# Code-book layer: for half of the sub-spaces the gates go through DRAM and come back with each row on 32 partitions

## The reference, cut to what matters

```python
B, T, D = (2, 512, 192)            # here the layer gets 16 tiles of 128 tokens, 2048 tokens in all
S, R, M, K = (8, 16, 64, 4)        # 8 sub-spaces of 16 features, 64 codes each, the best 4 are kept
H, G = (32, 64)                    # 32 hidden features per code
z = jnp.einsum('nd,sdr->nsr', xf, P)
scores = jnp.einsum('nsr,smr->nsm', z, C)
topv, topi = jax.lax.top_k(scores, K)
w = jax.nn.softmax(topv, axis=-1)
...
h = jax.nn.gelu(jnp.einsum('nsr,nskrh->nskh', z, W1g) + b1g)
yl = jnp.einsum('nskh,nskhr->nskr', h, W2g) + b2g
comb = jnp.einsum('nskr,nsk->nsr', yl, w)
out = jax.nn.gelu(comb @ G1 + g1b) @ G2 + g2b
```

## Time and profile before

| | before |
|---|---|
| median of 3 runs (lowest, highest) | 3582.79 us (3580.55, 3584.8) |
| profiled execution: own time | 3578.07 us |
| its span, first to last instruction | 3576.3 us |
| mean granted TensorE clock, share of full speed | 0.83 |
| PE, DVE, ACT busy over the span | 71%, 68%, 45% |
| loop over the 128 steps, about | 2291 to 2813 us |

### The profile page before, as it was taken

One profiled execution on the slowest core, in us unless ns is written; L12 is line 12 of the kernel. 1 busy time (PEld: TensorE's weight loads), 2 busy tenths in 40 slices (PEclk: granted clock), 3 DMA queues, 4 the chain that ended last, 5 costly groups with the idle time before them and its releaser, 6 DMA issues. The chain is left out here.

```text
span 3576.3 us, 39626 instructions
## 1 busy us (share of the span) xinstructions
PE 2556.9 (71%) x13085; PEld 1566.8 (44%) x13132; DVE 2419.3 (68%) x5733; ACT 1604.6 (45%) x2888; POOL 831.2 (23%) x438
## 2 busy tenths in 40 slices
PE   3968995788888876699831113788989777785466
PEld 3955663333434333499621111322222366664345
DVE  4454336399999997211378996687787699998621
ACT  1111112566666652111217772677777545554211
POOL 1000000467676762367200001000000011111021
PEclk9768997899999997799955555899999888887678
DMA  1121001202020200511100001000000100000221
GB/s 37 19 80 45 1 1 31 91 4 95 0 95 0 95 0 1 165 40 40 46 10 0 1 1 44 13 1 1 1 1 1 30 1 1 1 1 1 67 110 50
DMA packets 59444, 109.35 MB, mean 31 GB/s; under 512 B 32045, under 2 KB 47755, under 8 KB 53995
## 3 DMA queue, kind: packets, MB, share of 16 engines
q1 hardware_dynamic: 53484, 95.04, 8.2%
q0 software_dynamic: 5760, 11.82, 1.1%
HBM read 92.76 MB, written 18.03 MB: 31 GB/s over the span
## 5 line engine op out<-in xcount | busy, mean ns | idle before, releaser
L1938 POOL TENSOR_TENSOR mam_st<-mam_du,mam_b_rows 128x1536 f32<-128x1536 f32 x128 | 439.5, 3441 | 172.7 <-PE mam_ysum L2007 172.2
L2168 DVE TENSOR_TENSOR_SCAN mam_st<-mam_da,mam_st 128x512 f32<-128x512 f32 x384 | 441.0, 1204 | 35.9 <-ACT mam_da L2108 18.2
L1716 DVE TENSOR_TENSOR cod_hp<-cod_hp,cod_gate 128x512 f32<-128x512 f32 x512 | 324.2, 682 | 123.0 <-ACT cod_hp L1583 121.0
L2007 PE MATMUL mam_ysum<-mam_st,held_ident 128*128 128x512 f32 x768 | 391.5, 650 | 2.2 <-DVE mam_st L2174 2.2
L1583 ACT ACTIVATE cod_hp<-cod_up,cod_b 128x512 f32<-128x512 f32 x512 | 319.2, 693 | 130.7 <-PE cod_up L1454 130.1
L2108 ACT ACTIVATE mam_da<-mam_delta,mamw_decay 128x508 f32<-128x508 f32 x384 | 254.1, 683 | 184.2 <-DVE mam_st L2168 149.5
L2282 POOL TENSOR_TENSOR att_probs<-att_se,att_neg 128x1536 f32<-128x1536 f32 x16 | 55.0, 3440 | 999.7 <-DVE att_neg L2487 999.7
L2174 DVE TENSOR_TENSOR mam_st<-mam_st,mam_c_ps 128x1536 f32<-128x1536 f32 x128 | 224.4, 1753 | 16.9 <-PE mam_c_ps L2002 13.4
L2007 PEld LDWEIGHTS mam_ysum<-mam_st,held_ident 128*128 128x128 f32 x768 | 159.9, 208 | 168.6 <-issue 161.5
L489 DVE SCALAR_TENSOR_TENSOR held_h<-x_dn,held_gate,held_h 128x192 f32<-128x192 f32 x256 | 89.1, 410 | 183.8 <-PE x_dn L456 182.1
L1459 PE MATMUL cod_gate<-cod_wt,cod_sel_g 128*128 128x512 bf16 x465 | 181.6, 391 | 39.4 <-DVE cod_hp L1716 38.8
(11 more groups left out here) (523 smaller groups left out, 5484.2 us busy)
## 6 DMA issues: line engine op xcount, KB each, us to landing
mam_b_rows<-b_scratch SPq DMA_DIRECT2D x32, 1024.0 KB, 6.8
sw_w<-in_L_w SPq DMA_DIRECT2D x2, 4608.0 KB, 33.2
gr_w<-in_L_w SPq DMA_DIRECT2D x1, 5376.0 KB, 43.3
gr_w<-in_L_w SPq DMA_DIRECT2D x1, 4608.0 KB
slot_scratch<-in_slot_fresh SPq DMA_DIRECT2D x1, 3860.0 KB
gr_rows<-slot_scratch SPq DMA_DIRECT2D x40, 96.5 KB, 1.9
x1w_w<-in_L_w SPq DMA_DIRECT2D x1, 3072.0 KB
gr_w<-home_scratch SPq DMA_DIRECT2D x16, 192.0 KB, 4.4
```

The lines of the kernel that those rows point to most:

```text
L1716: nc.vector.tensor_tensor(at, at, gate[u % BANKS][:], ALU.mult).then_inc(gated, 1)
L1938: nc.gpsimd.tensor_tensor(st[it % N_ST][:], du[r % 2][:], along(b_rows[:, p % RING, n % PIECE, :], 1, [P, MC, MT]), ALU.mult)\
L2007: last = nc.tensor.matmul(ysum[:, c, :], m.ident[:], st[it % N_ST][:, c, :], start=False, stop=(it % DS == DS - 1))
L2168: nc.vector.tensor_tensor_scan(fs, fa, fs, 0.0, ALU.mult, ALU.add).then_inc(scanned, 1)
```

## The change

The sub-spaces of a step fall in two halves. For j = 0 and 1 (QP = 2) gates are made as before. For j = 2 and 3 (QD = 2) there is no gate matmul. Instead, once for each group:

- PE transposes the fp32 gates `ex` of these sub-spaces (`turn_gates`, eight 128 x 128 transposes, at k = 23 and 24), and ACT copies them to `turned_gates`, 128 x 2 x 512 fp32.
- SP stores them to DRAM, `gate_scratch[g % 2]`, by four DMAs of 64 rows x 2,048 bytes (`send_gates`, behind the bring of k = 28).
- SP brings, for each step, a buffer of `wide_gates`, 128 partitions x 4,096 bytes (512 KB), out of a ring of GRING = 5 (`bring_gates`). The source is listed as 4 codes x 32 repeats (stride 0) x 4,096 bytes, and the destination as 128 partitions x 4,096 bytes. A bring waits until the step five earlier is gated.
- DVE multiplies `hp` with `wide_gates` for j = 2 and 3, and waits for the bring's semaphore `gates_in`.

There are now 4 `up` banks and 2 `gate` banks. The splitting in bf16 parts runs over half as many columns, `turn_w` is done four times per group in place of eight (k = 25 to 28), and the second bias is added through `turned_gates` for the one half (`b2d`, two fp32 matmuls) and as before for the other. Group 0's gates are transposed and sent ahead of the loop. The raw first-layer weights are loaded into `wide_gates` in place of `wt[1]`.

```diff
-BANKS = 3
+BANKS = 4
+GBANKS = 2
 HOLD = 3
+QP = 2
+QD = QS - QP
+NSP = 2 * QP
+GRING = 5
+SEND_AT = 28
...
 def code_of(k, j):
-    return (k % HT + 2 * j) % HT
+    return (k % HT + 2 * j) % HT if j < QP else k % HT
...
+            def send_gates(g):
+                if g == 0:
+                    sp.wait_ge(first_kept, FIRST_GF + 2)
+                else:
+                    sp.wait_ge(misc_kept, prep_turn(g) + GF_AT + 2)
+                for half in range(2):
+                    for j in range(QD):
+                        sp.dma_start(m.gate_scratch[g % 2, half].rearrange("c e j t -> (c e) j t")[:, j],
+                                     turned_gates[j * SM:(j + 1) * SM, half, :]).then_inc(gates_out, 16)
+
+            def bring_gates(g, k):
+                step = g * STEPS + k
+                if step >= GRING:
+                    sp.wait_ge(gated, QS * (step - GRING + 1))
+                sp.dma_start(wide_gates[:, step % GRING].rearrange("p j t -> p (j t)"),
+                             along(m.gate_scratch[g % 2, k // HT, k % HT].rearrange("e j t -> e (j t)"), 1,
+                                   [ET, SH, QD * GT])).then_inc(gates_in[step % GRING], 16)
+
+            sp.wait_ge(w1_split, 1)
+            send_gates(0)
+            for g in range(NG):
+                sp.wait_ge(gates_out, 16 * 2 * QD * (g + 1))
+                for k in range(STEPS):
+                    bring_gates(g, k)
+                    if k == SEND_AT and g + 1 < NG:
+                        send_gates(g + 1)
...
+            def turn_gates(g, half, bank, ready):
+                pe.wait_ge(weighted, GS * (g + 1))
+                for t in range(GS):
+                    at = t * SS + half * QS + QP
+                    last = nc.tensor.transpose(bank[:, t * P:(t + 1) * P],
+                                               ex[:, at:at + QD, :].rearrange("p n e -> p (n e)"), m.ident[:])
+                last.then_inc(ready, 1)
...
-                if u >= BANKS:
-                    pe.wait_ge(gated, u - BANKS + 1)
+                if j >= QP:
+                    return
+                if u >= QS:
+                    pe.wait_ge(gated, u - QS + 1)
...
-                        if 24 <= k:
-                            keep(turn + WT_AT + k - 24, turned_to(g + 1, k - 24), turned_from(misc))
+                        if 23 <= k < 25:
+                            keep(turn + GF_AT + k - 23, turned_gates[:, k - 23, :], misc[:])
+                        if 25 <= k < 29:
+                            keep(turn + WT_AT + k - 25, turned_to(g + 1, k - 25), turned_from(misc))
...
                 v.wait_ge(h_ready, u + 1)
-                v.wait_ge(gate_ready, u + 1)
                 at = hp[step % HOLD][:, j, :]
-                nc.vector.tensor_tensor(at, at, gate[u % BANKS][:], ALU.mult).then_inc(gated, 1)
+                if j < QP:
+                    v.wait_ge(gate_ready, QP * step + j + 1)
+                    by = gate[j][:]
+                else:
+                    v.wait_ge(gates_in[step % GRING], 16 * (step // GRING + 1))
+                    by = wide_gates[:, step % GRING, j - QP, :]
+                nc.vector.tensor_tensor(at, at, by, ALU.mult).then_inc(gated, 1)
...
+        m.gate_scratch = nc.dram_tensor("gate_scratch", [2, 2, HT, ET, QD, GT], F32).ap()
```

More of the change, by code:

```diff
@@ L1322, in codes_stage @@
         w2 = s.sb("w2", [P, SS * HT, SR])
-        b2_part = [s.sb(f"b2_part{i}", [P, 2 * SS, 32], BF16) for i in range(NPART)]
+        b2_part = [s.sb(f"b2_part{i}", [P, 2 * NSP, 32], BF16) for i in range(NPART)]
+        b2d = s.sb("b2d", [P, 2, 32])
         g1 = s.sb("g1", [P, 2, SG])
@@ L1346, in codes_stage @@
         up = [s.psum(f"up{i}", [P, 512]) for i in range(BANKS)]
-        gate = [s.psum(f"gate{i}", [P, 512]) for i in range(BANKS)]
+        gate = [s.psum(f"gate{i}", [P, 512]) for i in range(GBANKS)]
         comb = s.psum("comb", [P, 512])
@@ L1356, in codes_stage @@
          comb_kept, b2_ready, dve, act_own) = (s.sem(n) for n in names)
-        N_IN = 9
+        gates_out = s.sem("gates_out")
+        gates_in = [s.sem(f"gates_in{i}") for i in range(GRING)]
+        N_IN = 10
         block = s.block()
@@ L1420, in turn_w @@
                 turned = bank[:].bitcast(BF16)
-                for n in range(SS):
-                    last = nc.tensor.transpose(turned[:, n * P:(n + 1) * P], cols[:, t * 2 * SS + h * SS + n, :],
+                for n in range(2 * NSP):
+                    last = nc.tensor.transpose(turned[:, n * P:(n + 1) * P], cols[:, t * 2 * NSP + n, :],
                                                m.bf_ident[:])
@@ L1455, in unit @@
                                  start=True, stop=True).then_inc(up_ready, 1)
[L1456 to L1457 removed]
+                if j >= QP:
+                    return
+                if u >= QS:
+                    pe.wait_ge(gated, u - QS + 1)
                 half, code = f // NBLK, f % NBLK
[L1459 removed]
+                nc.tensor.matmul(gate[j][:], sel_g[:, code, :], wt[g % 2][:, 2 * (QP * (k // HT) + j) + half, :],
                                  start=True, stop=True).then_inc(gate_ready, 1)
@@ L1467, in down @@
                     for q in range(2 * NPART):
[L1468 to L1471, removed]
+                        for j in range(QP):
+                            n = 2 * (QP * half + j) + q % 2
+                            nc.tensor.matmul(comb[32 * j:32 * j + 32, :], b2_part[q // 2][:, n, :],
+                                             wt[g % 2][:, n, :], start=(q == 0), stop=False)
+                    for j in range(QD):
+                        rows, at = slice(j * SM, (j + 1) * SM), 32 * (QP + j)
+                        nc.tensor.matmul(comb[at:at + 32, :], b2d[rows, half, :], turned_gates[rows, half, :],
+                                         start=True, stop=False)
                 pe.wait_ge(gated, QS * (step + 1))
@@ L1492, in _ @@
                 spread_w1(i, first_turn(first_w(i)))
-            for i in range(2 * GS):
-                turn_w(0, i, first_turn(FIRST_WT + i), first_ready)
+            for half in range(2):
+                turn_gates(0, half, first_turn(FIRST_GF + half), first_ready)
+            for t in range(GS):
+                turn_w(0, t, first_turn(FIRST_WT + t), first_ready)
             pe.wait_ge(first_kept, N_FIRST)
@@ L1607, in _ @@
                         high_w(0, t)
+            for half in range(2):
+                keep_first(FIRST_GF + half, turned_gates[:, half, :], lambda bank: bank[:])
             for t in range(GS):
                 mid_w(0, t)
-            for i in range(2 * GS):
-                keep_first(FIRST_WT + i, turned_to(0, i), turned_from)
+            for t in range(GS):
+                keep_first(FIRST_WT + t, turned_to(0, t), turned_from)
             act.wait_ge(w_in, 16 * N_IN)
```

49 lines of the change are left out of this document (29 added, 20 removed).

## The result

The changed kernel takes 3727.1 us (median of 4 runs, 3721.8 to 3732.1), the kernel before 3581.7 us in the same series (4 runs, 3579.5 to 3584.8). The ratio is 1.0405, with a 95% interval of 1.0389 to 1.0421. The forecast was 3712 us, range 3672 to 3810, with 0.84 on slower. The profiled run of the changed kernel is 3723.8 us long, with a span of 3721.9 us. The stage, from its first DMA issue to the next stage's first reduction, grew from 598.6 us (2222.91 to 2821.55) to 747.2 us (2219.08 to 2966.29), by 148.6 us; all other stages together are 3.0 us shorter.

What follows compares the result with a forecast made beforehand. Brings on 4 of 16 DMA engines were to bound the loop: start 2286 + 655.4 brings + 4.1 sends + 1.2 gating + 8.6 tail = 2955.3, +133.8 us on 3578.07, giving 3712 us, range 3672 to 3810.

Steps and rivals of the forecast that it cites:

- The mechanism: Brings: equal parts must cut source's 4 and destination's 128 at their outermost counts, so 4 of 16 DMA engines serve them.
- rival 1: Brings: cut by the destination's 128 over 16 engines, 1.2 us each; DVE bounds; 3491 us, -87 us; chance 0.15.
- The price of a bring: Each step's transfer: 32 rows on each of four engines, 160 ns per 4,096-byte row, 5.12 us.
- rival 2: Brings: 4 engines at the 108-row loads' 19.9 GB/s, 6.59 us each, 3900 us; chance 0.04 together with anything beyond 3810.
- first issue of the stage to the first step's gates: Stage's prologue: group 0's gates copied by 2281.4, stored, bring data flowing from 2286, then the first bring; 68.2 us.
- 127 steps at the regular pace: Loop: the brings' queue never empties, so every step takes a bring's 5.12 us; 650.2 us.
- stores and irregular steps: Loop at a group's change: three later sends cost only their bytes, 3 x 524,288 at 388 GB/s, 4.1 us.
- last gating to the next stage's first reduction: Stage's tail behind the loop: 8.6 us, as in the trace before the change.
- rival 3: PE's clock in the loop: hidden unless below 0.62; mean 0.6 adds 20 us, 3732 us; no chance of its own.
- SP's issues: SP issuing DMAs in the loop: some 0.5 us each, hidden.
- Five buffers, four brings always queued: Bring queue in the loop: five buffers keep four brings queued, so it never empties and the loop runs at its pace.
- 405 us of work, perhaps 30 of stalls: DVE over the loop if 16 engines serve the brings: 435 us in place of 522, -87 us.

Runs made afterwards that it cites:

- e1: Changed kernel with each bring cut into four DMAs of one code each (source 1 x 32 repeats), same bytes and rows: 3523.0 us, ratio 0.984 to the kernel before.
- e2: Changed kernel with each bring cut into two DMAs of two codes each, so each source list has an outermost count of 2: 4377.2 us (one run).
- e3: Changed kernel with the bring's source listed as 32 repeats x 4 codes, still one DMA, constants permuted alike: 3520.8 us, ratio 0.983 to the kernel before.
- e6: Changed kernel with brings of half the bytes: as many descriptors on 4 engines, each 2,048 bytes: 3523.1 us, ratio 0.984 to the kernel before.
- e5: Changed kernel with gates stored to DRAM for the first group alone, the later stores and SP's waits for them left out: 3730.5 us.
- e4: Changed kernel with one bring per group, 124 of 128 transfers left out, every step of the group using that buffer: 3523.3 us (one run).

## Why the prediction was right

**The mechanism** was right: the count of engines was read from the packets of DMAs with equal lists and carried to a pair of unequal ones, 4 and 128, by the argument that equal parts must cut both. e1, e2 and e3 show it for 1 x 32, 2 and 32. The trace of before could not exclude rival 1, since all its lists were cut alike; e3, which differs from the changed kernel in nothing else of the transfer than the order of the source's list, does. What isn't shown is the rule in full. In these pairs the source has the smaller or an equal count and every destination's count is a multiple of 16, so "the largest common divisor up to 16" and "the source's count, up to 16" give the same for them; the 13 and 12 of the earlier trace rows speak for divisors, and a destination with the smaller count was not tried.

**The price of a bring** was put at 5.12 us and measures 5.08: 131,072 bytes per engine in 5.08 us are 25.8 GB/s, between the 24.3 and 26.6 GB/s of the earlier trace rows. It rested on the right neighbours, and the straight line through them held (e6). The bound of 6.59 us from the 108-row loads was far off, as was judged, and rival 2 with it.

**The sum** was 133.8 us for the stage, against 148.6 measured. It fell short by 14.8 us, in four terms (the two units behind the last step's gates, 1.2 us put and 1.3 measured, are not listed):

| term | predicted | measured | difference |
|---|---|---|---|
| first issue of the stage to the first step's gates | 68.2 | 73.8 | +5.6 |
| 127 steps at the regular pace | 650.2 | 645.2 | -5.0 |
| stores and irregular steps | 4.1 | 14.2 | +10.1 |
| last gating to the next stage's first reduction | 8.6 | 12.7 | +4.1 |

The first row is a sum of small things: the gates are copied 0.8 us later than put, the stores land later by about 1.6 us, and the first bring, issued at 2283.49, is gated at 2292.91, 9.4 us later, where 0.9 + 5.1 us were put. Of the 9.4, 1.4 us pass before its first packet and 7.3 until its last mark. The -5.0 of the second row takes back a quarter of what the others add. The third row is the term that was mis-sized. It held the stores alone, which was right for them (3 to 4 us by e5), and took every other step as regular. Of the 14.2 us, 3.9 are the steps 28, 60 and 92, the stores; 7.8 are eight single steps, told of in the last section; the remaining 2.4 are the net of steps at long preparation and the shorter ones behind them. The last row is rival 3's clock at a place where I hadn't looked for it. The down matmuls behind the last gating, eight of them, took 1.05 us in the earlier trace rows; here:

```profile
2953.69 1.91 PE L1528 MATMUL cod_comb<-cod_hp,cod_w 128*16 128x512 f32 x8 [3.16 <-DVE cod_hp L1782]
```

The granted clock of this stretch is 0.50, 1.2 GHz in place of 2.4, and it stays there to the stage's end, where the kernel before has 1.00:

```profile
2955.70:2966.30 10.60, 6.94 (x12) 3.03 (x12) 1.11 (x3) 1.24 (x2) 0.00 (x0) 0.50 0.00 0
```

PE had been idle for 3.16 us ahead of these matmuls. The matmuls of the tail take 1.91, 3.65, 1.65 and 1.65 us, and took 1.05, 1.90, 0.92 and 0.92: together 4.1 us more, the whole of the row. Inside the loop the slower clock is hidden, as argued: the mean granted clock is 0.85, PE is busy 477 of 668 us. But behind the loop nothing hides it, and the tail is paid at the low clock.

**SP's issues** were put at 0.5 us each and hidden. They are hidden, but they aren't 0.5 us long (last section). "Five buffers, four brings always queued" was not quite so; about three and a half were, which was enough.

**Rival 1's size** was wrong. It was put at -87 us, 3491; e1, e3 and e4 give -61 to -64 against their own series of before, e6 -57. The step that failed is "405 us of work, perhaps 30 of stalls": in e3's loop (2296 to 2752 us) DVE is busy 391 of 456 us, so the work is 14 us less and the stalls are 65 us. In e3, ACT still waits 83 us for PE's `up` and DVE 70.5 us for ACT, in steps of 4 to 7.5 us into which preparation for the next group falls. Had the forecast been rival 1, its range of 3465 to 3530 would have held the time, near its end.

## What to carry to other kernels

Before a DMA is called hidden, count the engines that will serve it: for the lists of this kernel, the largest number up to 16 that divides the outermost count of the source and of the destination. (Whether it is the divisor or the smaller count for unequal lists, these runs don't separate.) For a broadcast onto partitions, put the repeat outermost and pay with a permutation of constants that is made once; that took 206 us from this kernel. Where constants can't be permuted, one DMA for each row, so that the repeat is all that is left of the list, took 204 us (e1), at four times the issues. In a trace, a DMA share that is flat at 4/16 or 2/16 while someone waits for the transfer is the sign of it, and packets less rows, divided by the DMAs, confirm it.

## What the runs showed of the hardware beside this

**Issues block when a queue is full.** SP's first five brings in the changed kernel wait for no buffer. Their issues take 0.6, 0.5, 0.5, 3.1 and 5.5 us (start, duration):

```profile
2283.49 0.61 SPq L1406 DMA_DIRECT2D cod_wide_gates<-gate_scratch  x1
...
2285.26 3.08 SPq L1406 DMA_DIRECT2D cod_wide_gates<-gate_scratch  x1
...
2288.38 5.47 SPq L1406 DMA_DIRECT2D cod_wide_gates<-gate_scratch  x1
```

In e3, with the same rows on 16 engines, the fifth takes 0.62 us:

```profile
2294.79 0.62 SPq L1406 DMA_DIRECT2D cod_wide_gates<-gate_scratch  x1
```

So with four engines the queue takes about three brings, some 100 descriptors on each engine, and then the issuing engine stands. In e6, with as many descriptors of half the bytes, the fourth takes 0.72 us and the fifth 1.54:

```profile
2295.14 1.54 SPq L1406 DMA_DIRECT2D cod_wide_gates<-gate_scratch  x1
```

There SP stands with at most 5 x 64 KB handed to an engine, while the changed kernel's first three issues hand over 3 x 128 KB without standing. The limit is therefore not one in bytes. Nor is it one in DMAs, by the five of e3, none of which had landed (the first did at 2296.23 us). Descriptors fit all: counted from issues less packets, an estimate, 113 to 123 are outstanding on each engine when a long issue of the loop's first dozen ends in the changed kernel and in e2, 120 and 135 in e6, and under 45 in e3. In the changed kernel the median issue takes 4.88 of a step's 5.08 us: SP looks like the busiest of all, and is only held up by the four engines. On SP nothing else was waiting. From ACT or POOL the same DMAs could have held up work of those engines; no run here tried it.

**Single steps longer by about 1 us.** Eight steps of the changed kernel (27, 40, 48, 57, 71, 87, 103 and 119) are 0.6 to 1.3 us longer than 5.08 without a store or long preparation as the reason; the last two are in the last group, which has no preparation at all. In all eight a packet of the instruction-fetch queue q14 is on the DMA engines (for step 48 it comes 0.2 us after the step's start), which is so in only 20 of all 127 steps; in e5 it is so in ten of the eleven steps over 5.5 us. The DMA counts from 2829 to 2834 us, in one such step of the last group:

```profile
q1 hardware_dynamic: 124, 0.49, 25.2%
q14 instruction: 1, 0.01, 0.4%
```

The trace's records of single packets show why some of the twenty matter and others don't:

- Behind eleven of them, the next two rows on the queue take 0.50 and 0.47 to 0.49 us, in place of 0.16. All eight long steps are among these, and in the last group no other rows take 0.4 us or more. The fetch (0.33 us) and what the two rows take too long (0.34 and 0.33) come to 1.0 us; the two steps of the last group, 103 and 119, are 0.97 and 1.29 us longer.
- Behind eight others the two rows take about 0.32 and 0.38 us, 0.7 us too long in all with the fetch, and the steps stay at 5.08 where no long preparation is near (56, 70, 84, 98 and 114).
- The marks tell the two kinds apart. The gating starts 0.57 us behind the mark of the engine that ends a bring last. At steps 87 and 103 that mark is the late one, 6.06 us behind the one before it. At 84, 98 and 114 it comes after 5.08 us, and marks on which nothing waits are late, by 0.7 us at 84 and 114.
- In e2, where two engines carry the brings, packets of the second kind have the slow rows behind them, and six steps (42, 55, 70, 83, 98, 113) are 0.68 us longer. At the first kind's places its steps are regular.

So a fetch delays the rows of an engine on which it falls, by its own time and that of two slow rows, and it delays the step where that engine is the last to finish. That the two kinds are packets on two different engines is argued from this, since the records don't name the engine, and no run took the fetches away. A transfer on 16 engines has a quarter of the bytes on each and was hidden in any case.
